# Adding x through an identity matmul in the output product of the sampling stage, with the copy to x on ScalarE

## The reference

```
x = x + L0_attention(layernorm(x), ctx)      # correlation by Fourier transform, top 4 shifts
x = x + L0_ffn(layernorm(x))                 # a product with a folded matrix, plus bias
x = x + L1_attention(layernorm(x), ctx)      # deformable sampling, then out @ w_out + b_out
x = x + L1_ffn(layernorm(x))                 # quantised gate/up/down product
```

## Time and profile before

| | |
|---|---|
| three runs | 1158.2, 1158.79, 1163.41 us |
| the profiled execution, its own time | 1156.88 us |
| its span from the first to the last instruction | 1155.1 us |
| PE busy | 958.9 us, 83% |
| DVE busy | 735.5 us, 64% |
| ACT busy | 506.3 us, 44% |
| POOL busy | 280.9 us, 24% |
| mean granted TensorE clock | 0.926 |

### The profile page before, as it was taken

The page is one execution under the profiler, slowest core; times in us unless marked ns, Lnnn a source line. Parts: engine busy times, 40 slices in busy tenths (PEclk is TensorE's granted clock), DMA queues, the critical chain, the costliest instruction groups (busy, mean ns, idle before and its releaser), DMA issues.

```text
span 1155.1 us, 13450 instructions
## 1 busy us (share of the span) xinstructions
PE 958.9 (83%) x4829; PEld 600.2 (52%) x4829; DVE 735.5 (64%) x1246; ACT 506.3 (44%) x853; POOL 280.9 (24%) x251
## 2 busy tenths in 40 slices
PE   1399998899797977678888889699958866994998
PEld 1277776688575666334444445344423322442887
DVE  4377777454573666547888888645329995787333
ACT  0132321311122433356666666134379962764332
POOL 0200000122103111147788777201001100100000
PEclk8699999999898988859999999799989997996999
DMA  9500000000000000000000000000000000000111
GB/s 322 197 1 1 1 1 1 1 1 1 10 1 1 1 1 1 1 0 1 1 1 2 1 2 1 1 0 1 1 0 0 1 0 0 0 0 1 41 51 56
DMA packets 18236, 20.25 MB, mean 18 GB/s; under 512 B 1201, under 2 KB 17531, under 8 KB 18046
## 3 DMA queue, kind: packets, MB, share of 16 engines
q1 hardware_dynamic: 12950, 12.86, 3.4%
q10 hardware_dynamic: 5224, 6.57, 1.7%
HBM read 15.22 MB, written 4.19 MB: 17 GB/s over the span
## 4 chain that ended last, share of the span: by engine, by line
PE 36%; DVE 12%; POOL 6%; ACT 5%; issue 2%; ACTq 0%; DVEq 0%
PE pair L1120 15%; PE pair L1151 7%; POOL hat L528 4%; PE pair L1040 3%; PE pair L1054 3%; DVE peak L1577 2%; DVE wide L1573 2%; DVE peak L1563 2%; PE pair L1016 2%; PE pair L1024 1%; ACT down_b L712 1%; DVE sig L1568 1%; ACT wide L753 1%; DVE hat L1440 1%; PE pair L1066 1%
## 5 line engine op out<-in xcount | busy, mean ns | idle before, releaser
L1120 PE MATMUL pair<-xqs,wuT 128*128 128x512 f32 x384 | 173.1, 609 | 19.7 <-DVE peak L1563 19.0
L528 POOL TENSOR_TENSOR hat<-hat 128x1024 f32<-128x1024 f32 x62 | 145.6, 2359 | 45.7 <-DVE hat L1440 44.9
L1120 PEld LDWEIGHTS pair<-xqs,wuT 128*128 128x128 f32 x384 | 73.6, 195 | 117.8 <-issue 82.8
L1024 PE MATMUL pair<-rows,sel 32*128 32x512 bf16 x256 | 75.4, 398 | 23.0 <-ACT down_b L712 17.4
L1440 DVE SCALAR_TENSOR_TENSOR hat<-pair,down_a 128x1024 f32<-128x1024 f32 x64 | 78.1, 1221 | 24.1 <-PE pair L1016 19.7
L553 POOL CAST xqs<-xqT 128x1024 f32 (+1 forms) x24 | 26.3, 1094 | 269.4 <-PE pair L1120 191.8
L1151 PE MATMUL pair<-wdT,hid 128*128 128x256 f32 x384 | 85.7, 388 | 2.9 <-DVE hid L1607 2.9
L1440 DVE SCALAR_TENSOR_TENSOR hat<-pair,down_b 128x1024 f32<-128x1024 f32 x64 | 78.1, 1220 | 12.0 <-PE pair L1016 11.7
L712 ACT ACTIVATE down_b<-pair 128x512 f32<-128x512 f32 x128 | 69.4, 595 | 37.0 <-PE pair L1024 32.1
L1120 PE MATMUL pair<-xqs,wgT 128*128 128x512 f32 x192 | 85.1, 601 | 0.0
L712 ACT ACTIVATE down_a<-pair 128x512 f32<-128x512 f32 x128 | 69.5, 595 | 33.2 <-PE pair L1024 23.7
(11 more groups left out here) (207 smaller groups left out, 1859.9 us busy)
## 6 DMA issues: line engine op xcount, KB each, us to landing
x_sb<-in_x_dram SPq DMA_DIRECT2D x8, 512.0 KB, 11.9
c_sb<-in_ctx_dram SPq DMA_DIRECT2D x8, 512.0 KB, 17.0
out_dram<-x_sb SPq DMA_DIRECT2D x16, 256.0 KB, 2.1
four<-in_c_four_dram ACTq DMA_DIRECT2D x1, 1280.0 KB, 12.4
deq<-in_L_ffn_w_gate_dram ACTq DMA_DIRECT2D x1, 768.0 KB, 12.5
deq<-in_L_ffn_w_up_dram ACTq DMA_DIRECT2D x1, 768.0 KB, 16.0
deq<-in_L_ffn_w_down_dram ACTq DMA_DIRECT2D x1, 768.0 KB, 16.2
big<-in_c_big_dram ACTq DMA_DIRECT2D x1, 448.0 KB
```

The source lines that it names most:

```text
L528: nc.gpsimd.tensor_tensor(hat[:, n % RING, :], hat[:, (n - 2) % RING, :], hat[:, n % RING, :], ALU.add).then_inc(summed, 1)
L1024: mm(bank[6 + i], sel[g:g + 32, pp, 1, :], rows[g:g + 32, q, c * 2 + a, :], start=True, stop=True).then_inc(down_mm, 1)
L1120: last = mm(bank[2 + oc][:], w[:, c, oc * 128:(oc + 1) * 128], xqs[:, s, c, :], start=(c == 0), stop=(c == DC - 1))
```

## The change

Inside the output product, behind the bias and ahead of the four matmuls with `w_out`, PE multiplies the identity matrix by the two sequences of x and accumulates into the same bank. The bank then holds the new x itself. ACT copies it to `x_sb` and reports `x3_done`; it does so in the loop behind the relus of t = 7 and 11, and for quad 7 after the loop. DVE's addition goes.

```diff
@@ scalar
+                if n >= TURN and n % TURN in (7, 11):
+                    keep_x3(n // TURN - 1, n % TURN // 11)
+
+            def keep_x3(q, i):
+                act.wait_ge(out_mm, 2 * q + i + 1)
+                two = q * QUAD + 2 * i
+                nc.scalar.activation(x_sb[:, two:two + 2, :], bank[5].rearrange("p (b d) -> p b d", b=2), ACT.Copy).then_inc(x3_done, 1)
...
             keep_attT(NQ - 1, 1)
+            keep_x3(NQ - 1, 0)
+            keep_x3(NQ - 1, 1)
@@ tensor, project_att
                 mm(bank[5][:].rearrange("p (b d) -> p b d", b=2), ones3,
                    bias3[:, BAT["bout"]:BAT["bout"] + D].unsqueeze(1).broadcast_to([3, 2, D]), start=True, stop=False)
+                two = q * QUAD + 2 * i
+                mm(bank[5][:].rearrange("p (b d) -> p b d", b=2), IDN, x_sb[:, two:two + 2, :], start=False, stop=False)
@@ vector
-                if q and t in (7, 11):
-                    add_out(q - 1, t // 11)
...
-            def add_out(q, i):
-                dve.wait_ge(out_mm, 2 * q + i + 1)
-                xb = x_sb[:, at(q * QUAD + 2 * i, 2), :]
-                V.tensor_tensor(xb, bank[5][:].rearrange("p (b d) -> p b d", b=2), xb, ALU.add).then_inc(x3_done, 1)
...
             for i in range(2):
-                add_out(NQ - 1, i)
                 two_moments(NQ - 1, i)
```

## The result

The changed kernel takes 1168.85 us (median of four runs, 1168.78 to 1204.05) against 1158.49 us for the kernel before in the same comparison (1156.2 to 1163.41): a ratio of 1.0083, 95% interval 1.0043 to 1.0124. It is slower, as forecast; 1172.4 was foretold, and 1165 to 1178 as the range. Four executions that took over 1.5% more than the fastest of their kernel, at a lower mean granted clock, are part of no ratio: the one of 1204 us here, one of 1205 us of e1 and two of 1179 us of e4 further down. Of the execution that was profiled the time is 1168.9 us and the span 1167.0, 11.9 us more than before.

The account below looks back on a forecast made before the run. The bound was taken to be a chain through POOL, then TensorE with short ACT pieces, not any full engine. 12.0 us in the loop plus 1.5 behind gave +13.6, forecast 1172.4 us, range 1165 to 1178.

Parts of the forecast that it names:

- The bound: Sampling stage: a repeating turn of 27.29 us, a chain of waits holding both output products; no engine full over it.
- two halves: Turn's chain: through POOL from pair 14 to the next turn's pair 5, then through TensorE with short ACT pieces to pair 14.
- Identity, 0.86 each: Output product on PE: each added f32 identity matmul costs 0.86 us, nothing hides it; 12.0 us for 14 in the loop.
- bounds of 0.77 and 1.12: Lower and upper bound, in us, on what PE pays for one identity matmul in the output product.
- DVE's additions, 0 in the loop: Removing 14 DVE additions of 0.68 us at pairs 7 and 11 gives the chain nothing; bound on the other side 4.8 us.
- Rival 2: DVE's relief lets the second product start earlier and gives 4.8 us back: +8.8 us, 1167.6; chance 0.11.
- the full stretch: DVE is busy 7.00 of 7.00 us from 624.50 to 631.50, called the best argument for the change.
- ACT's copy, covered: ACT's 0.60 us copy fits between product end P and the next relu at P + 0.57, 0.05 to spare: 0 us.
- Rival 3: ACT becomes late: the copy pushes the relu of pair 12 by 0.5 us: +17.1 us, 1175.9; chance 0.15.
- Rival 1: Identity matmul streams one column per cycle like the bf16 bias, 0.21 us each: +3.2 us, 1162.0; chance 0.03.
- Rivals 4 and 5: DVE paces the turn, 1149.1, chance 0.04; POOL is the true pace and absorbs PE's lengthening, 1160.3, chance 0.04.
- Sum: Whole kernel: 12.0 us in the loop plus 1.5 behind it, +13.6 us, 1170.5 from the profiled execution; chance 0.63.

Follow-up runs that it names:

- e1: Changed kernel, but DVE instead of ACT copies the sum to x, identity matmul kept; turn 29.03 us, ratio 1.0092 to the kernel before.
- e4: Changed kernel with one bf16 matmul of the same shape in place of each f32 identity matmul; turn 27.52 us, ratio 0.9986 to the kernel before.
- e3: Changed kernel with two identity matmuls in each product instead of one; turn 30.71 us, ratio 1.0217 to the kernel before.
- e2: Changed kernel without the identity matmul, ACT copying the output product alone; turn 27.27 us, ratio 0.997 to the kernel before.
- e6: Changed kernel with `take` (t = 9) and the clearing product (t = 13) moved ahead of the down-products; turn 28.68 us, ratio 1.0079 to the kernel before.
- e12: Changed kernel, bias and identity issued early at t = 5 and 9, clearing product of t = 13 moved; turn 26.98 us, ratio 0.9993 to the kernel before.
- e11: Kernel before, its bias matmuls issued early at t = 5 and 9, clearing product of t = 13 moved; turn 26.69 us, ratio 0.9941.
- e7: Changed kernel with bias and identity issued early for both products (t = 5 and 9); turn 27.94 us, ratio 1.0113 to the kernel before.
- e9: Changed kernel with bias and identity issued early for the first product alone (t = 5); turn 28.56 us, ratio 1.0221 to the kernel before.
- e10: Changed kernel with bias and identity issued early for the second product alone (t = 9); turn 28.39 us, ratio 1.0166 to the kernel before.
- e8: Changed kernel, bias and identity early at t = 5 and 8, `take` and clearing product moved ahead; turn 28.27 us, ratio 1.0059 to the kernel before.

## Why the prediction was right

- **The bound.** The chain was read rightly. Both products of a turn stand in it, and each microsecond put into them comes out of the turn (e3). The two halves are real: in every kernel without an early identity matmul at t = 5 POOL's half is 12.23 to 12.25 us in the turns of the table, while PE's half goes from 14.45 to 18.46. That POOL's work is what fills its half is read from the chain; no run changed that work.
- **Identity, 0.86 each.** Measured 0.86 net (chain, e2 to e3). The bounds of 0.77 and 1.12 weren't reached: 1.12 was a record with its fill, and the gap behind the bias stayed (L1062 starts 0.31 us behind L1059).
- **DVE's additions, 0 in the loop.** 0.02 us a turn (e2). Rival 2, up to 4.8 us given back, is out, and with it the argument from the full stretch: a stretch without idle time for an engine doesn't make it the bound if another is level with it. The 0 belongs to this order of PE's work: it is 0.17 a turn in e6 and some 0.39 in e12, where PE no longer takes the gain back.
- **ACT's copy, covered.** The relu starts at P + 0.57 as before; the reserve was 0.05 by my working and it was enough. Rival 3 is out; against DVE's addition or copy ACT's copy is worth 0.02 to 0.04 us a turn.
- **Rival 1** (one column per cycle for any type), the rule of the Trainium skill's page TensorE: Matmul & The Clock Gate, fits the 0.21 us of the bf16 bias and not f32, where the trace has 0.86 us for 512 columns.
- **Rivals 4 and 5**: the turn grew by 1.70; neither DVE nor POOL took it in. Rival 4's sum was also wrong in itself: it left out the two identity matmuls behind the loop, where nothing covers them. With them it is 1158.8 - 9.5 + 1.5 = 1150.8, not 1149.1.
- **Sum.** 12.0 in the loop: 11.8. 1.5 behind it: 1.5. 13.6 in all: the first spreading of a scale comes 14.2 us later, 0.8 of it from ahead of the loop, so 13.4.
- **What was off.** I took the stages behind as only shifted, and named a change in their length as a sign of being wrong; it came. In the profiled executions they were 2.3 us shorter, 1.6 of it where the clock came back sooner, against 0.8 more at the start. So 11.9 instead of 13.6, 1168.9 instead of 1170.5. The other 1.9 us of the forecast came from setting the sum on the median of the runs of before, which spread over 7 us; the changed kernel's profiled time lies at its own median, so nothing was to be added for it. With these two the result lies under the forecast's own 1170 to 1175 and next to the 1167.6 of rival 2. By the time alone the two can't be told apart; the turn does it: 28.99 us, where 29.0 was foretold and 0.68 less would have been rival 2's.
- **A sign that was foretold wrong.** L1054 was to start about 1.15 us behind the bias and started 1.27 behind (627.60 to 628.87). By the rows it then took 0.10 us less than before (1.89 against 1.99): 1.27 - 0.30 - 0.10 = 0.87, the same net price.

## What to carry to other kernels

Moving an addition onto the tensor engine as an identity matmul isn't free because it is "in the same accumulation": in f32 it cost four times what bf16 did, here 0.86 us for 512 columns. It can pay only where the engine that it relieves is in the chain, and TensorE isn't. No run here had it pay: even in e12, where DVE's relief counted, the kernel was slower than e11 without it. Before moving work off an engine, look for it in the chain of waits; a stretch in which it never idles isn't proof. If the matmul must be added, issue the parts of the group that need no late operand (bias, residual) where TensorE waits for someone: with that and the moved clearing product the exchange went from 1.70 to 0.29 us a turn. Then time the whole kernel: in e7, e9 and e10 the turns got shorter and the falls of the clock took all of that back, or more.

## What the runs showed of the hardware that I had not expected

- In the middle of a busy stage the granted clock fell from 1.00 to 0.50 for about 20 us in the profiled executions of e7, e9 (twice) and e10 (PE 23.9 of 26 us busy in e9 before it), while those of e8 and e12 kept 1.00 at 24.4 to 25.2 of 26. So the fuller engine was not the one that lost its clock. e11 has two short falls of about 3 us (its turn of quad 4 is 28.27 us instead of 26.69), and its timed runs lie in two groups, 1149.8 to 1151.0 and 1156.2 to 1156.6; the traced one is of the second. Each kernel has one trace, and two of e12's ten runs were 11 us slower without one. Whether the order of the work or something beside it decides is left open; no run here tells the two apart.
- A bf16 matmul of 512 columns in front of an f32 group cost 0.12 us net, less than the 0.21 us that the bias of the same width holds the chain: it takes 0.24 and saves 0.10 of weight load behind it. An f32 one takes 0.97 and saves the same 0.10, so net prices (0.12 and 0.86) are not in the ratio of the passes, gross ones are.
